# Sums and half sums of three weight matrices: from VectorE to GpSimd, in a fused Perceiver block on one core

## What is computed

```python
x = x + xattn(layernorm(x), ctx, ctx, mask, Wq, bq, Wk, bk, Wv, bv, Wo, bo)   # 16 heads of 32, 257 context rows
x = x + mix(layernorm(x), Wq, bq, Wk, bk, Wv, bv)                             # q, k, v = x @ W + b;
                                                                              # s = sum over tokens of bind(k, v);
                                                                              # out = unbind(s, q), both by rfft/irfft
x = x + experts(layernorm(x), W1, W2, Wg, bg)                                 # 8 experts of 512 x 2048, the best one per token
```

## Time and profile before

| | us |
|---|---|
| median of 3 runs (lowest, highest) | 804.28 (803.01, 804.78) |
| the profiled execution | 809.27 |
| span in its trace | 807.3 |
| TensorE busy in the span | 775.0 |
| VectorE busy | 624.6 |
| ScalarE busy | 471.0 |
| GpSimd busy | 242.6 |
| mean granted TensorE clock | 0.983 |

### The profile page before, as it was taken

How to read it: one execution, slowest core, us unless ns; L and a number is a source line. 1 busy time by engine, 2 the same in 40 slices (tenths; PEclk the granted TensorE clock), 3 DMA queues, 4 the chain that set the end, 5 groups by cost and what they waited for, 6 DMA issues and landing times.

```text
span 807.3 us, 22183 instructions
## 1 busy us (share of the span) xinstructions
PE 775.0 (96%) x8851; PEld 460.1 (57%) x8851; DVE 624.6 (77%) x990; ACT 471.0 (58%) x847; POOL 242.6 (30%) x413
## 2 busy tenths in 40 slices
PE   8989999999999999999999999995999999999995
PEld 3445545555445555455557544554967866876783
DVE  4977888879788888787768668788778788778860
ACT  4546666656665565665547133238568758857960
POOL 0235234433354433344430200012153241331220
PEclk9999999999999999999999999996999999999998
DMA  8324453344413345323523511104899988998500
GB/s 306 140 64 109 106 155 94 80 107 108 94 41 93 94 107 134 64 71 106 122 55 57 209 53 53 53 0 137 287 386 415 405 348 290 350 350 301 230 31 15
DMA packets 94901, 125.56 MB, mean 156 GB/s; under 512 B 76352, under 2 KB 79168, under 8 KB 83956
## 3 DMA queue, kind: packets, MB, share of 16 engines
q1 hardware_dynamic: 92260, 117.65, 45.6%
q0 software_dynamic: 2576, 7.02, 2.4%
HBM read 100.47 MB, written 6.88 MB: 133 GB/s over the span
## 4 chain that ended last, share of the span: by engine, by line
PE 81%; DVE 11%; ACT 3%; DMA 2%; issue 1%; POOL 1%; SPq 1%; POOLq 0%; DVEq 0%; ACTq 0%
PE bank L1474 60%; PE bank L1852 10%; PE bank L1643 4%; DVE arena L933 3%; PE bank L1824 3%; PE bank L1609 3%; ACT arena L695 2%; DVE arena L989 1%; DMA arena<-arena 1%; DMA arena<-in_wv_t 1%; DVE arena L995 1%; ACT arena L662 1%; PE bank L1811 1%; DVE arena L948 1%; DVE arena L965 1%
## 5 line engine op out<-in xcount | busy, mean ns | idle before, releaser
L1474 PE MATMUL bank<-arena 128*128 128x160 f16 (+8 forms) x3944 | 562.9, 303 | 8.2 <-DVE arena L1366 2.0
L1474 PEld LDWEIGHTS bank<-arena 128*128 128x128 f16 (+2 forms) x3944 | 322.4, 100 | 236.6 <-issue 13.8
L662 ACT ACTIVATE arena<-arena 128x256 f16<-128x256 f32 (+5 forms) x302 | 254.1, 889 | 21.8 <-PE bank L1824 7.9
L933 DVE SCALAR_TENSOR_TENSOR arena<-arena 128x2048 f16<-128x2048 f32 (+4 forms) x102 | 200.5, 1987 | 37.5 <-ACT arena L662 34.6
L662 ACT ACTIVATE arena<-bank 128x512 f16<-128x512 f32 x175 | 100.1, 584 | 144.4 <-PE bank L1474 110.6
L933 DVE SCALAR_TENSOR_TENSOR arena<-bank,arena 128x512 f16<-128x512 f32 x174 | 116.8, 682 | 44.4 <-ACT arena L662 40.8
L1852 PE MATMUL bank<-arena 128*128 128x512 f16 x384 | 86.6, 379 | 0.0
L695 ACT ACTIVATE arena<-arena 128x257 f32<-128x257 f32 x128 | 63.5, 498 | 21.9 <-DVE arena L997 21.9
L528 POOL TENSOR_TENSOR arena<-arena 32x1024 f16<-32x1024 f32 (+1 forms) x16 | 34.1, 2132 | 140.1 <-PE bank L1643 139.9
L1852 PEld LDWEIGHTS bank<-arena 128*128 128x128 f16 x384 | 36.1, 98 | 41.1
L545 POOL COPY arena<-arena 32x256 f16 (+1 forms) x128 | 50.3, 393 | 24.0 <-DVE arena L933 11.8
(11 more groups left out here) (112 smaller groups left out, 486.1 us busy)
## 6 DMA issues: line engine op xcount, KB each, us to landing
arena<-in_w SPq DMA_DIRECT2D x64, 1024.0 KB, 6.8
arena<-in_ctx_t SPq DMA_DIRECT2D x15, 1024.0 KB, 5.4
arena<-in_awt SPq DMA_DIRECT2D x3, 1024.0 KB, 7.1
l_dram<-arena SPq DMA_DIRECT2D x4, 512.0 KB, 4.4
x_dram<-arena SPq DMA_DIRECT2D x1, 2048.0 KB, 13.7
arena<-in_wk_t SPq DMA_DIRECT2D x4, 256.0 KB, 4.8
arena<-in_ctx_t SPq DMA_DIRECT2D x4, 256.0 KB, 6.8
arena<-in_wv_t SPq DMA_DIRECT2D x1, 1024.0 KB, 8.2
```

What stands on the lines that cost most here:

```text
L662: return a.activation(dst, src, ACT.Copy, scale=scale)
L933: return v.scalar_tensor_tensor(dst, src, scale, h, ALU.mult, ALU.subtract)
L1474: last = m.matmul(out_ap, w, x, start=(n == 0), stop=(n == len(pairs) - 1))
```

## The change

`weight_sums` and `weight_half_sums` go from VectorE's stream to GpSimd's, word for word but for the engine. There they stand behind GpSimd's `step(st)` of the same steps. So that they can, GpSimd's loop over pairs of steps is written out as 14 steps.

```diff
--- before.py
+++ after.py
@@ -575,11 +575,28 @@
             last_keys(0, 1)
             query_hi(KC + 3)
             queries_of(1)
-            step(1)
-            with pool.Fori(1, STEPS // 2 - 1) as k:
-                for par in range(2):
-                    step(k * 2 + par)
-            step(STEPS - 2)
+            def weight_sums(k):
+
+                pool.wait_ge(s[f"wt_landed{k}"], 16)
+                g.tensor_tensor(wt_sum, wt_a[k], wt_b[k], ALU.add).then_inc(s["wt_sums"], 1)
+                pool.wait_ge(s["wt_sums"], 2 * k + 1)
+                g.tensor_tensor(wt_b[k], wt_a[k], wt_b[k], ALU.subtract).then_inc(s["wt_sums"], 1)
+
+            def weight_half_sums(k):
+
+                pool.wait_ge(s["wt_sums"], 2 * k + 2)
+                for n, (dst, z) in enumerate(((wt_a[k], wt_sum), (wt_sum, wt_b[k]))):
+                    if n:
+                        pool.wait_ge(s["wt_halves"], 2 * k + 1)
+                    g.tensor_tensor(dst[:, 0], z[:, 0], z[:, 1], ALU.add)
+                    g.tensor_tensor(dst[:, 1], z[:, 0], z[:, 1], ALU.subtract).then_inc(s["wt_halves"], 1)
+
+            for st in range(1, STEPS - 1):
+                step(st)
+                if st in SUM_STEPS:
+                    weight_sums(SUM_STEPS[st])
+                if st in HALF_SUM_STEPS:
+                    weight_half_sums(HALF_SUM_STEPS[st])
             step(STEPS - 1, nxt=False)
             attention_rows(STEPS - 1, last=True)
 
@@ -1091,22 +1108,6 @@
                 dve.wait_ge(s["bias_landed"], 16)
                 v.tensor_tensor(x_tok[:, n], x_tok[:, n], bias_tile, ALU.add).then_inc(s["x_biased"], 1)
 
-            def weight_sums(k):
...
-            def weight_half_sums(k):
...
             def mixing_weights_lo(k, n):
 
                 dve.wait_ge(s["wt_hi"], 2 * k + n + 1)
@@ -1183,10 +1184,6 @@
 
             for st in range(1, STEPS - 1):
                 step(st, st % 2, mixing=mixing_of(st))
-                if st in SUM_STEPS:
-                    weight_sums(SUM_STEPS[st])
-                if st in HALF_SUM_STEPS:
-                    weight_half_sums(HALF_SUM_STEPS[st])
                 for n in BIAS_TILES.get(st, ()):
                     add_bias(n)
             step(STEPS - 1, 1, nxt=False)
```

## The result

The changed kernel takes 820.58 us (median of 4 runs, 820.52 to 821.89), the kernel before 804.53: a ratio of 1.0205, interval 1.0191 to 1.0219.

The account below looks back on a forecast made before the run. TensorE, almost alone, bounds the attention stage, with VectorE's adds barely hidden. Three sum steps at 1.40 us plus three half-sum steps at 2.55 give 11.85 us; added to the 804.28 us median: 816.1 us, range 809.5 to 822.

Parts of the forecast that it names:

- The two edges: VectorE's last `p_lo` (transposes just in time) and last `k_lo` (0.25 us before scores); each microsecond beyond them stands on TensorE.
- The sum steps: Steps 1, 4, 7: GpSimd's adds delay VectorE's `p_lo` 1.57 us, 0.17 is free; loss 1.40 us each.
- The port's turns: VectorE and GpSimd operations on two SBUF operands exclude each other and alternate; hand-over 0.13 us before the first ends.
- the rival without it, 811.1 us: No port exclusion for these adds: sum steps lose nothing, half-sum steps 2.26 us each; 811.1 us, chance 0.15.
- stricter rule: Shared port: the first comer holds it for its whole instruction; the sum would be about 15.0 us instead of 11.8.
- The half-sum steps: Steps 2, 5, 8: half sums 2.80 us later through ScalarE's wait to the scores, less 0.25; loss 2.55 us each.
- L528 starts at 99.82 and later: GpSimd idles 9.28 us per step before L528, covering the adds and the written-out loop, which cost nothing there.
- The clock rival: TensorE's clock also falls in half-sum steps, 1.7 us each; all three give 821.2 us, one 817.8; chance 0.25.
- a sign of being wrong: Attention stage, 60 to 430 us: granted clock expected at 1.00; wrong if the clock rows show 0.50.
- The "not slower" rival: ScalarE's wait at L762: costs nothing if GpSimd's four half sums finish within 2.47 us; 803.8 us, chance 0.05.
- the 0.16 us stalls: Kernel before: TensorE loses about 0.16 us in each of three half-sum steps, 0.5 us in all.

Follow-up runs that it names:

- sums_only: Changed kernel with the half sums back on VectorE, only the two 128x1024 adds per matrix on GpSimd: 808.48 us, ratio 1.0048.
- half_after_plo: `half_only` with GpSimd's four half-sum adds made to wait until `p_lo` of the step is done: 827.16 us, ratio 1.0286.
- half_rows_late: `half_only` with ScalarE's two row copies, which wait for the half sums, moved behind `k_hi(3)`: 808.40 us, ratio 1.0055.
- sums_dodge: `sums_only` with two waits on GpSimd: first add after `p_lo` of the step, second after VectorE's split of the next context: 803.26 us, ratio 0.9994.
- late_values: Changed kernel with GpSimd's L528 of steps 3, 6, 9 waiting until VectorE has made the mixing matrix's low half: 821.94 us, ratio 1.0206.
- after: The changed kernel itself, all sums and half sums on GpSimd, against the kernel before: 820.58 us, ratio 1.0205.
- half_only: Changed kernel with the 128x1024 sums back on VectorE, only the four half sums per matrix on GpSimd: 816.29 us, ratio 1.0151.
- late_fillers: `late_split_loop` plus matmuls nobody reads in TensorE's two waits of steps 3, 6, 9: 821.01 us, ratio 1.0208.
- late_split_loop: The control: `late_values` with TensorE's loop broken up so that steps 3, 6, 9 stand alone, no fillers: 821.12 us, ratio 1.0204.
- unroll: Kernel before with GpSimd's loop over step pairs written out, all sums left on VectorE: 804.17 us, ratio 0.9996.
- all_rows_late_dodge: Changed kernel with both the waits of `sums_dodge` and the ScalarE order of `half_rows_late`: 808.59 us, ratio 1.0062.

## Why the forecast held, and where it was short

**The two edges.** They are where the time went. The views named both before the change was run: transposes just in time, `k_lo(3)` 0.25 us ahead of the scores. `sums_only` crosses the first alone (+4.4), `half_after_plo` the second alone (+23.0, of which 19.5 are waits and some of the rest the halved clock), `half_rows_late` takes the second away and keeps the first (+4.2).

**The sum steps** were forecast at 1.40 us each and are 1.61, 1.76 and 1.79 us longer than before. The adds took 2.35 us against 2.24 from the two rows of f16 outputs, and the second 2.42 with its wait for the port. L501 was 0.20 in these steps, as forecast for the case without VectorE's add beside it.

**The port's turns** came as worked out from one collision: GpSimd, VectorE, GpSimd, VectorE, and then VectorE's rest. That `sums_dodge` loses nothing, with the same adds, shows that their meeting is the cause, and a `p_lo` of 0.47 us that takes 2.58 beside an add is exclusion; the rival without it, 811.1 us, is ruled out. By the Trainium skill's stricter rule (SBUF — State Buffer, "Who interferes with whom"), the port held for the whole instruction, the sum would have been 15.0 by the prediction's estimate (its own steps, done again with that rule, give 14.6). That is nearer to the measured loss, but not for its reason, and this trace does not agree with the rule to the letter: behind the second half-sum add, which ends at 115.75, the first `p_lo` ends at 116.03, and so, if it took its usual 0.47 us, it ran from 115.56. The hand-over comes 0.19 us before the recorded end.

**The half-sum steps** are the term that was too small: 2.55 us each was forecast, and they are 4.05, 3.87 and 4.78 us longer than before. Up to the scores the mechanism and nearly the size were right: waits of 1.49 and 1.38 us in the first, 2.87 together (2.85 and 3.14 in the others). The surplus of 0.3 us is that of the adds: the half sums were ready 5.33 us after the first began (113.25 to 118.58) where 5.02 was forecast, since an f32 add of 512 elements takes 1.27 us, not the 1.156 of the row taken for it. The step that failed is "L528 starts at 99.82 and later", by which everything behind the adds on GpSimd was to be covered and was put at nothing. I had asked how long GpSimd may be busy ahead of L528, but not whom L528 would meet at the port once TensorE's block had moved against VectorE's conversions. In the kernel before, VectorE's low half of the mixing matrix came first, and nobody waited for L528. Now L528 comes first and VectorE loses 1.1 us in each of the three steps, of which TensorE loses 0.93 in the two at full clock. With L528 held back the low half takes 1.21 us again, and no step at full clock has that wait: one in `late_values` (27.81 us), one in the control (27.75), two with fillers (27.50 and 27.49).

**The range** was wide enough, but not for this cause. Its upper end of 822 stood there for the strict port rule and for the clock; the collision at L528, 1.9 us, and the longer adds had no place in it. That 820.58 fell inside is in part luck.

**The clock rival** was neither the whole cause nor absent. The prediction named halved clock in the stage as a sign of being wrong, and the sign came, once. In the attention stage of the profiled executions the granted clock fell once in after, `half_only` and `late_fillers`, twice in `late_values` and `late_split_loop`, three times in `half_after_plo`, and never in `unroll`, `sums_only`, `half_rows_late`, `sums_dodge` and `all_rows_late_dodge`, which leave TensorE at most one wait in a step. In the profiled execution of after it cost about 1.7 us and spared a wait of 0.93, 0.8 in all. In the median of after it can have cost little: the mean granted clock of its four executions is 0.983 to 0.985, that of the kernel before 0.982 to 0.986, and 0.001 of it is worth 0.8 us (an estimate: the span times the missing share, if TensorE is always busy). Whether it is what ate the 2.8 us that `late_values` should have gained is not proven: its trace says so for two steps, and so does its one execution of 817.54 us, but the times of the kernels with and without fillers did not part.

**The sum again.** The six steps are 17.9 us longer (5.2 and 12.7) in the two profiled executions, against 16.0 us between the medians and a forecast of 11.8. Of the 6.0 us between 17.9 and the 11.85 forecast, 1.0 is in the sum steps, whose adds were longer, 1.9 in the collisions at L528 (2 x 0.93), 1.2 in waits longer than 2.55 (0.3, 0.3 and, with a later transpose, 0.6) and 1.7 in the clock; 0.2 is assigned to nothing. The 17.9 us are more than the medians' 16.0 in part because the executions differ outside of the steps: against that of `unroll`, 1.3 us of them are given back there. The remaining 0.6 is open. The "not slower" rival needed GpSimd's half sums within 2.47 us; they took 5.33. Its price, like the 0.16 us stalls in the prediction's first paragraph, was set a little low: the three half-sum steps of the kernel before stand 0.17, 0.34 and 0.26 us above 24.39, 0.8 in all and not 0.5.

## What to carry to other kernels

Before work is moved from VectorE to GpSimd, find for each operation moved, and for those behind it on GpSimd, which of VectorE's operations with two SBUF operands will be issued beside it, and who waits for those; that GpSimd is idle and nobody needs the result soon says nothing. The same adds at the same length cost 4.4 us where they met `p_lo` and nothing where two semaphore waits kept them apart. And look at the order of the waiting engine's queue: half sums that came some 3 us late (ScalarE idled 4.19 us for them in place of 1.13) did that part of their harm only because three conversions that TensorE needed stood behind it.

## What the runs showed of the hardware

- GpSimd's f32 adds on 128 partitions took 1.26 to 1.27 us for 512 elements and 2.35 for 1024 where nobody held the port. The subtraction L588, with f16 output and one f16 operand, took 1.156 for 512; which of the two makes the difference was not tested.
- The profile counts the wait for the port as busy time of the waiting instruction: an operation of 0.47 us shows as 2.58, and VectorE's busy time rose by 3.9 us though 15.6 us of work had left it.
- TensorE's granted clock fell to 0.50 (1.2 GHz) for 3.4 or 6.8 us in or just behind the second of two idle stretches of about 1.5 and 1.3 us with a half block between them, in 6 of the 12 such steps traced (`after`, `half_only`, `late_values`, `late_split_loop`); in a single wait of 6.4 to 6.7 us it fell each time, before the wait had ended. In the stage, no trace of these kernels shows a fall behind a single wait of 1.5 to 1.8 us.
- The hand-over of the port between the two engines came 0.13 to 0.19 us before the recorded end of the operation that held it, worked out by counting the other's usual length back from its end: 0.19 from GpSimd to VectorE in the two steps shown above, 0.13 in the earlier trace rows, and 0.13 from VectorE to GpSimd at L583, which took 2.42 us in place of 2.35.
- VectorE's operations with one operand in PSUM did not lengthen beside GpSimd's: in the changed kernel 23 conversions of 128x512 out of PSUM (L950, `arena<-bank,arena`) ran over 0.3 us beside one of GpSimd's tensor operations and took 0.675 to 0.694 us, the other 157 took 0.674 to 0.694. The one at 125.34, beside L528, is shown above.
